# Identity products in TensorE's pauses of a post-norm decoder kernel

## The reference

```
x = LN(x + self_attention(x))              16 heads of 16, 4 KV heads, RoPE, causal
x = LN(x + latent_cross_attention(x, ctx)) 16 heads, latent 64 + rope 64, banded mask
x = LN(x + experts(x))                     16 experts, top 4, plus a shared one
x = LN(x + gated_delta_rule(x))            16 key heads, 32 value heads of 128
x = LN(x + int8_cross_attention(x, ctx))   w8a8 projections for q and the output
x = LN(x + top1_shared_kv_attention(x))    one of 16 heads' k and v for all queries
```

## Time and profile before

| | us |
|---|---|
| median of 3 runs | 2323.47 |
| lowest, highest | 2316.97, 2324.92 |
| profiled execution | 2323.68 |
| its span, first to last instruction | 2321.7 |
| busy in it: PE, PEld, DVE, ACT, POOL | 1972.4, 1435.0, 1455.9, 843.4, 157.3 |

### The profile page before, as it was taken

The page is one execution under the profiler, slowest core; times in us unless marked ns, Lnnn a source line. Parts: engine busy times, 40 slices in busy tenths (PEclk is TensorE's granted clock), DMA queues, the critical chain, the costliest instruction groups (busy, mean ns, idle before and its releaser), DMA issues. The chain is left out here.

```text
span 2321.7 us, 26545 instructions
## 1 busy us (share of the span) xinstructions
PE 1972.4 (85%) x9860; PEld 1435.0 (62%) x9860; DVE 1455.9 (63%) x3232; ACT 843.4 (36%) x1348; POOL 157.3 (7%) x147
## 2 busy tenths in 40 slices
PE   6988987898995878998989999899998984777786
PEld 4868777554553557586675866757567572455464
DVE  3667665224222667867778676776767764767666
ACT  2434433111111544344443535444344421333243
POOL 2011010100002000000000000000000002012010
PEclk8989899899996889999999999999999996777786
DMA  3000000500002210202102021030210202000000
GB/s 133 6 14 10 6 5 5 192 0 10 0 0 89 39 37 13 53 19 46 38 15 51 28 37 38 15 70 10 37 38 20 45 1 73 8 12 15 7 5 5
DMA packets 132528, 72.14 MB, mean 31 GB/s; under 512 B 109808, under 2 KB 122672, under 8 KB 131408
## 3 DMA queue, kind: packets, MB, share of 16 engines
q1 hardware_dynamic: 132400, 70.44, 11.7%
HBM read 57.13 MB, written 13.11 MB: 30 GB/s over the span
## 5 line engine op out<-in xcount | busy, mean ns | idle before, releaser
L1286 PE MATMUL c_bank<-c_Y,c_NP 128*128 128x128 f32 x1536 | 179.5, 277 | 20.9 <-ACT c_Y L1439 20.9
L1286 PEld LDWEIGHTS c_bank<-c_Y,c_NP 128*128 128x128 f32 x1536 | 174.9, 192 | 26.5 <-issue 26.5
L1604 DVE TENSOR_TENSOR c_Y<-c_V,c_bank 128x512 f32<-128x512 f32 x192 | 131.8, 686 | 86.0 <-PE c_bank L1286 86.0
L1210 PE MATMUL c_bank<-c_xT,c_wqk 128*128 128x512 f32 x256 | 126.5, 641 | 3.7 <-ACT c_pad L1402 3.1
L1542 DVE SCALAR_TENSOR_TENSOR c_cv<-c_pad,c_wcqk,c_cv 128x1024 f32<-128x1024 f32 x96 | 122.2, 1279 | 9.5 <-ACT c_cv L1416 8.7
L1542 DVE SCALAR_TENSOR_TENSOR c_cv<-c_pad,c_wcv,c_cv 128x1024 f32<-128x1024 f32 x96 | 122.5, 1283 | 2.6
L1579 DVE SCALAR_TENSOR_TENSOR c_NP<-c_NP,c_cj,c_bank 128x256 f32<-128x256 f32 x256 | 104.8, 475 | 29.8 <-ACT c_NP L1445 29.8
L1362 PE MATMUL c_bank<-c_wout,c_yT 128*128 128x256 f32 x512 | 120.4, 381 | 0.0
L1278 PE MATMUL c_bank<-c_NP,c_Tb 128*128 128x256 f32 x512 | 116.0, 383 | 0.0
L1167 POOL TENSOR_TENSOR c_V<-c_Y 128x512 f32<-128x512 f32 x32 | 39.9, 1248 | 1115.4 <-ACT c_Y L1439 1115.4
L1210 PE MATMUL c_bank<-c_xT,c_wv 128*128 128x512 f32 x256 | 111.9, 595 | 3.6 <-DVE c_acc L1632 3.6
(11 more groups left out here) (406 smaller groups left out, 3942.2 us busy)
## 6 DMA issues: line engine op xcount, KB each, us to landing
b_wup<-b_in_wup SPq DMA_DIRECT2D x4, 1280.0 KB, 13.3
c_wqk<-c_in_wqk SPq DMA_DIRECT2D x9, 512.0 KB, 3.2
c_wv<-c_in_wv SPq DMA_DIRECT2D x8, 512.0 KB, 3.3
c_wz<-c_in_wz SPq DMA_DIRECT2D x8, 512.0 KB, 4.6
c_wout<-c_in_wout SPq DMA_DIRECT2D x8, 512.0 KB, 3.5
diagonal_blocks<-c_NP SPq DMA_DIRECT2D x64, 64.0 KB, 2.0
c_A<-diagonal_blocks SPq DMA_DIRECT2D x8, 512.0 KB, 3.7
c_NP<-no_blocks SPq DMA_DIRECT2D x32, 128.0 KB, 4.5
```

The source lines that it names most:

```text
L1210: last = pe.matmul(four(pair[q][:, :]), w[:, c * P:(c + 1) * P], xT[:, c, 4 * q:4 * q + 4, :], start=c == 0, stop=c == DC - 1)
L1286: last = pe.matmul(banks[n % 4][:, b * P:(b + 1) * P], lhsT(h, 4 * q + b), rhs(h, 4 * q + b), start=True, stop=True)
L1604: dve.tensor_tensor(rr(Y, h, q), rr(V, h, q), four(banks[n % 4][:, :]), ALU.subtract).then_inc(s["y_ready"], 1)
```

## The change

A helper issues a given number of products of the f32 identity by the identity repeated four times (128x512) into a PSUM bank whose contents aren't needed; nothing reads them. It is called ahead of certain waits of PE: in the attention stages, and ahead of the first two `values` of each round. Where the bank could still be read by another engine, a wait for that reader stands ahead of the call. Counts, by place:

- layer 0: 5 at the start; in each pass, for lane 0 only, 11 ahead of the self-attention's scores, 5 ahead of L461, 2 ahead of the cross scores; for both lanes 1 behind the self-attention.
- delta rule: 20 ahead of `values(0, 0)`, 3 ahead of it in the later rounds, 4 ahead of `values(i, 1)`.
- layer 1: 8 at the start; in each pass 4 and 7 (lane 0, lane 1) ahead of L1933; 1 in both lanes behind the cross-attention, 4 and 3 ahead of the second L1905, 1 in both behind the self-attention; for lane 0 only 11 ahead of L1956, 5 ahead of L1973, 3 ahead of the self scores.

```diff
+def keep_busy(pe, times, bank, ident):
+    for _ in range(times):
+        pe.matmul(four(bank[:, :]), ident, spread(ident, 4), start=True, stop=True)
...                                   # layer 0 attention, TensorE
+            pe.wait_ge(consts, 1)
+            keep_busy(pe, 5, lanes[0].O, ident[:, :])
             pe.wait_ge(weights, 16 * (len(shapes) - len(factors)))
-            pe.wait_ge(consts, 1)
...
             def lane_program(i, L, more):
+                if L.n == 0:
+                    if i:
+                        pe.wait_ge(L.ln2.step, at(i - 1, L.ln2.DVE_STEPS, 1))
+                    keep_busy(pe, 11, L.T, ident[:, :])
                 pe.wait_ge(L.kr_ready, at(i, 2, 2))
...
                 yield from L.self_att.on_tensor(pe, i, self_scores, lambda n, h: L.vaug[:, n, :])
+                keep_busy(pe, 1, L.S, ident[:, :])
                 pe.wait_ge(L.self_att.o_done, at(i, QUADS, QUADS))
...
+                if L.n == 0:
+                    keep_busy(pe, 5, L.S, ident[:, :])
                 pe.wait_ge(L.ln1.done, i + 1)
...
+                if L.n == 0:
+                    keep_busy(pe, 2, L.O, ident[:, :])
                 pe.wait_ge(L.seg_step, at(i, 4, 4))
...                                   # delta rule, TensorE
             def values(i, n):
-                pe.wait_ge(s["silu_ready"], at(i, CHUNKS, QK + n + 1))
                 if n == 0:
                     pe.wait_ge(s["pad_ready"], at(i, 2 * CHUNKS, 2 * (QK + 1)))
+                    keep_busy(pe, 3 if i else 20, banks[4], ident[:, :])
+                if n == 1:
+                    pe.wait_ge(s["z_ready"], at(i, B, B))
+                    keep_busy(pe, 4, banks[6], ident[:, :])
+                pe.wait_ge(s["silu_ready"], at(i, CHUNKS, QK + n + 1))
...                                   # layer 1 attention, TensorE
+            pe.wait_ge(s["consts"], 1)
+            keep_busy(pe, 8, lanes[0].O, ident[:, :])
             pe.wait_ge(s["weights"], 16 * len(shapes))
-            pe.wait_ge(s["consts"], 1)
...
             def project8(i, L, n, out):
                 yield
+                if n:
+                    keep_busy(pe, (4, 3)[L.n], L.S, ident[:, :])
                 pe.wait_ge(L.xquant.done, at(i, 2, n + 1))
...
                 yield from project8(i, L, 0, L.M[:, D:2 * D])
                 yield
+                if i:
+                    pe.wait_ge(L.self_att.o_done, at(i - 1, QUADS, QUADS))
+                keep_busy(pe, (4, 7)[L.n], L.O, ident[:, :])
                 pe.wait_ge(L.yb_ready, at(i, 2, 1))
...
                 yield from L.cross_att.on_tensor(pe, i, cross_scores, lambda n, h: L.vaug[:, 4 * n + h, :])
+                keep_busy(pe, 1, L.S, ident[:, :])
...
+                if L.n == 0:
+                    keep_busy(pe, 11, L.S, ident[:, :])
                 pe.wait_ge(L.ln1.done, i + 1)
...
+                if L.n == 0:
+                    keep_busy(pe, 5, L.S, ident[:, :])
                 pe.wait_ge(L.krep_ready, i + 1)
...
+                if L.n == 0:
+                    keep_busy(pe, 3, L.S, ident[:, :])
                 pe.wait_ge(L.vaug2_ready, i + 1)
...
                 yield from L.self_att.on_tensor(pe, i, self_scores, lambda n, h: L.vaug2[:, :])
+                keep_busy(pe, 1, L.S, ident[:, :])
```

## The result

| | before | after |
|---|---|---|
| median (us), runs | 2321.37, 4 | 2362.95, 4 |
| lowest, highest | 2316.97, 2324.92 | 2349.88, 2371.23 |
| ratio, 95% interval | | 1.0173 [1.0151, 1.0196] |
| span of the profiled execution | 2321.7 | 2348.1 |
| mean granted clock in it | 0.90 | 0.961 |

What follows compares the result with a forecast made beforehand. TensorE bounds the delta rule; in the attention stages the chain alternates between TensorE and VectorE. Overrun pauses less half clock saved: layer 0 +5, delta rule +1, layer 1 +26, so 2323.7 + 32 = 2355.7 us; own range 2345 to 2367.

Steps and rivals of the forecast that it cites:

- The price: Each added f32 matmul call is two records and costs 0.86 us at full clock, 1.71 at half clock.
- cheap: Rival, chance 0.10: a call takes 0.43 us, all groups fit their pauses, half clock behind them goes; -48, 2276 us.
- Layer 0: First attention stage: added calls overrun pauses, partly repaid by full clock; +5 us, from -3 to +14.
- Delta rule: First round +4.9 us from overrun, seven later rounds together -4.2; sum +1, from -8 to +6.
- Layer 1: Last attention stage, holding most of the loss: +26 us, from +13 to +45.
- query groups: Layer 1, four and seven calls ahead of the query transposes: net +1.3 to +1.5 four times, +5.6 us.
- tails and eleven: Layer 1, calls after the cross-attention and eleven ahead of L1956: net +5.8 twice, +4.0 twice, +19.6 us.
- five and three: Layer 1, calls behind the eleven: covered by VectorE, while half clock up to L1981 shrinks; -3.7 us.
- end pairs: Layer 1, one call per lane at the self-attention's end, no wait to fill: +1.5 three times, +4.5 us.
- Full clock through the tails: Rival, chance 0.20: the clock stays full behind cross- and self-attention tails; -14, 2342 us.
- Half clock on the added work: Rival, chance 0.10: added groups run long at 1.71 us a call; +15 likely, +34 at most in layer 1; 2371 us.
- Does nothing: Rival, chance 0.04: added matmuls are dropped, or their clock effect and delay both vanish; 2323.5 us.

Runs made afterwards that it cites:

- the fitted one with 5 at the start of layer 1: Changed kernel with fewer calls, as many as fit each pause, none behind the attentions, 5 at layer 1's start: 2274.65 us, 0.9798 of the kernel before.
- eleven ahead of the norm: Against the fitted one with 5 at the start of layer 1: 11 calls instead of 6 ahead of layer 1's norm transposes; 2292.93 us.
- three more groups: Against the fitted one with 5 at the start of layer 1: calls added at three more places in the delta rule's rounds; 2271.08 us.

## Why the prediction was right, and where its steps were off

The forecast was 2355.7 us, with its mechanism: calls of 0.86 us, too many for their pauses. The median is 2363.0. In the sum of +32 the profile has +26.

*The price.* 0.86 at full clock is what each group shows. The trace agrees with four passes for f32 (the Trainium skill, "FP8 and Floating Point Precision", TensorE Precision Notes): 0.86 is about four times the 0.22 from the bf16 L2014 to the line behind it (2124.23 to 2124.45). The rival "cheap" needed 0.43 a call; made so by half the columns, it came out faster, as it said, but at 2293 instead of 2276. It had taken all pauses as filled and all half clock behind them as gone; neither held. With 0.86 at +42 and 0.43 at -28 us the sign changes near 0.60 us a call, if it is linear, not at 0.69.

*Layer 0:* +5 predicted, +7.5 measured. The first input transposes come 2.2 late, 1.1 of it from ahead of the first added call (a later start and more half clock) and 1.0 from the five calls, as predicted. From the start of a pass (the first: from the stage's first instruction, itself 0.3 late) to its fifth scores the eleven give +1.5, +2.6, +2.7 and +2.0 for 0, +2.3, +2.3 and +1.7; what followed gave back 1.7 for 1.2. The start's gain covered less of the first pass than I took.

*Delta rule:* +1 predicted. The first round is +4.9, as worked out (L1269 ends at 824.51 by its row, not at 824.35, which moves nothing by more than 0.2), and the other rounds take 24.93 for 24.9. Their saving is 2.7, not 4.2, as the last round, which has no next projection to speed up, loses 0.6. The step that failed is one I had not made: that the rest of the round stays as it is. Alone, the groups cost 6 us. Of these, 2.2 lie in the stretch that I summed and 3.5 in that rest, in their profiles. The profile of after nevertheless shows -4.5 for the stage; 3.3 us of it come from the clock at the start of the stage, ahead of this stage's added calls. Behind the same wait of 20.8 us the same 32 records took 7.07 us before and 3.76 after. Two other kernels have the same instructions as each other up to that place: the fitted one with 5 at the start of layer 1, which took 3.76 as well, and that with eleven ahead of the norm, which took 7.06. So these 3.3 us differ from execution to execution, and that they fell to after is luck (the lines are of before, after and eleven ahead of the norm).
```profile
732.60 7.07 PE L1186 MATMUL c_bank<-c_wba,c_xT 128*128 128x64 f32 x32 [0.78 <-ACT c_xT L1383]
```
```profile
739.03 3.76 PE L1202 MATMUL c_bank<-c_wba,c_xT 128*128 128x64 f32 x32 [0.78 <-ACT c_xT L1403]
```
```profile
720.61 7.06 PE L1202 MATMUL c_bank<-c_wba,c_xT 128*128 128x64 f32 x32 [0.78 <-ACT c_xT L1403]
```

*Layer 1:* +26 predicted, +24.2 measured, for partly other reasons. In the profiles it divides so:

| part | predicted | measured |
|---|---|---|
| start, to the first L1905 | 0 | -0.4 |
| query groups, from L1905 to the cross-attention's first products with the values (L156) | +5.6 | +5.7 |
| tails and eleven, from there to the last L1968 ahead of the keys' transposes | +19.6 | +19.9 |
| five and three, from there to the self-attention's first products with the values (L156) | -3.7 | -1.0 |
| end pairs, from there to the next L1905 | +4.5 | 0 |

Pass by pass the tails and the eleven give +5.4, +6.2, +2.9 and +5.5, the five and three -0.9, -0.5, -0.6 and +1.0; of these I had three at -1.4 and one at +0.9, which is -3.3 and not the -3.7 of my sum. For these I had let TensorE's stretch shrink by its clock; but between the norm and the row maximum the path is VectorE's router chain and quantization, which no clock of TensorE shortens: in the second pass of after the critical chain is on VectorE from 2112.75 to 2127.97. The calls were covered as predicted, most of the gain was not there. The end pairs, in the second pass, make the projections behind them (L1946, before L1923) 1.8 us later, which these give back at full clock, as before had half clock there. In the fitted kernel, which has little half clock there, the same pairs cost 9 over three passes. The two misses, 2.7 too low and 4.5 too high, largely cancel: that the stage came within 2 us is in part luck.

*Full clock through the tails* did not hold throughout: in the second pass the calls behind the cross-attention ran at 0.73, and in three of the four passes some 3.5 us at half clock fall into these calls. *Half clock on the added work* has something in it for these calls, but not for the eleven, which run at 0.86 each. *Does nothing* is out.

*The median* lies 7 us above the forecast, the profiled execution 6 below it. The sum was made from one execution of before, whose runs differ by 8 us; those of after differ by 21. Between the medians the change is +41.6 us where the sum has +32. The delta rule may give 5 of the missing 10, since its groups alone cost 6.0 between medians where I had 1: that the rest of a round keeps its length is the step that I had left out. The longer falls at the sums of squares explain 7 us between two profiles of after. The three executions of after without a profile have mean clocks of 0.948 to 0.953 instead of 0.961, which makes, as an estimate, 40 to 60 us more at half clock, and take 12 to 21 us longer; where these falls lie is open.

## What to carry to other kernels

A filler on an in-order engine is worth something only up to the pause: size it by the pause in the trace divided by what one call takes (here two records, 0.86 us), count what else the waiting group waits for (here 20.9 of 28.9 us passed before the filler's operand existed), and put none where nothing waits. The same idea with the counts fitted to the pauses was 2.0% faster than before (2.2% with three more groups), with the counts too large 1.7% slower. Ask of each piece at full clock whether TensorE or another engine was the path there.

## What the runs showed of the hardware

TensorE's busy time doesn't tell its clock. Products of 17 columns filled 15.37 of 15.70 us and the clock stood at 0.55; with 512 columns in the same pause, ahead of the norm's transposes, it was full. The Trainium skill ("TensorE: Matmul & The Clock Gate", Why this matters for your kernels) advises to keep TensorE busy; by that the narrow calls should have served as well as the wide ones, and here the measurement decides against it, by 83 us.

Filling one pause doesn't take away the falls of the clock elsewhere. With the pauses of the values filled, the falls at the one-column sums, later in the round, stayed, and in seven of nine profiles they were 3.5 to 9 us longer over seven rounds; two profiles of one kernel differ there by 7 us. With calls right ahead of the sums these ran at full clock, 24.6 us over seven rounds instead of 35.4.

Half clock differs between executions where the instructions don't: the same 32 records behind the same wait of 20.8 us took 3.76 us in one profile and 7.06 in another.
